# Feed-forward portions and the output projection inside the attention, issued as four products of 32 array columns each

## The chip, the cores and the metric

The kernel runs on one NeuronCore of one Trainium2 chip. The metric is the time of one execution on the device in microseconds. Three runs of the kernel before took 2801.73, 2804.95 and 2811.61 us, a median of 2804.95 us.

## The reference, cut to what matters

x has the shape (4, 2048, 256), float32: four batches of 2048 tokens.

```
xn  = layernorm(x)
x1  = layernorm(xh  + mha(xh,  wq1, wk1, wv1, wo1))      # xh: the first 128 features of xn
x2  = layernorm(xsh + mha(xsh, wq2, wk2, wv2, wo2))      # xsh: the same of holt(xn), a smoothing over the tokens
y   = concat(x1, x2)
out = x + layernorm(y + relu(y @ w_ff1.T + b_ff1) @ w_ff2.T + b_ff2) + relu(xn @ W1 + b1) @ W2 + b2

mha: 8 heads of 16 features; softmax(q k^T / 4) v over all 2048 tokens, the heads side by side, then @ wo.T + bo
```

Each batch has so two attentions of 8 heads, a small network on y (256 to 1024 to 256), and a second, independent one on xn (W1, W2). The change concerns the products of that second network and those with wo.

## The kernel before, in words

**Stages.** For each of the four batches there is a prologue (transposes, projections to q, k and v, the smoothing), the attention of both branches, and the network on y (`nets`). Every engine has its own program, and semaphores tie them together. The middle batches are one loop (`Fori`).

**The attention.** A batch is cut into 16 units (2 branches x 2 groups of 4 heads x 4 chunks of 512 query tokens), and a unit into 16 steps over the key tiles of 128 tokens (kt). In `attention` of `tensor_program` TensorE issues, in this order, for each step kt:

- the scores of step kt + 1 (L1160): 4 products, each with 50 array rows and 128 columns, two of them side by side in the upper and the lower half of the array rows;
- in half of the steps one portion of the second network: in the even units `second_hidden` (L1031), 6 products that make 128 of the 1024 hidden features for 256 tokens; in the odd units `second_out_part` (L1045), 6 products of the second matrix. Each product has all 128 array rows and columns, 256 streamed columns and float16 operands (a value is split into a high and a low part, so three pairs of parts times two halves of the contraction or two hidden blocks);
- in step 8 of each unit but the first, `out_projection` (L1016) of the unit before: 4 products of 128 x 128 on 128 streamed columns in float32, each of which is two instructions in the trace;
- the values of step kt (L1184): for each of the 4 heads one product of 128 array rows and 17 columns (16 features and a column of ones for the sum) on 512 streamed columns, in float32, again two instructions each. Head j writes to the PSUM partitions from 32 j on, so the four lie side by side in the array columns.

The steps with a portion are `NET_KTS` = 0, 2, 4, 6, 10, 12, 14 and 15 (in unit 0 of a batch `FIRST_NET_KTS`), and the projection is in `PROJECTION_KT` = 8. So steps 14, 15 and the next unit's 0 have portions without a step between them.

**What couples the engines.** ScalarE makes one exponential of 128 x 1024 for each half of a step's scores (L584), two per step. The scores cycle through three PSUM slots and the exponentials through four SBUF buffers. The scores of half n wait for the exponential n - 3, and the values of step kt for both exponentials of that step. VectorE takes the portion's result out of the bank `side` (`hidden_half`, L719 to L723; `second_tile`, L731), reads the values of a finished unit (`evict`, L676) before the first values of the next unit may overwrite them, normalises them, and adds the projection to the residual (L713). In its program the work on the last portion of an even unit stands ahead of `evict`.

**Weights.** Each product has a weight load of its own, a separate instruction (PEld in the profile). A matmul's left operand is what is loaded, its right operand what is streamed.

Of the kernel before, what the change touches and what calls it, by code (L numbers as in the profile page):

```python
# [6 lines left out]
B, S, D = 4, 2048, 256  # L7
# [5 lines left out]
P = 128  # L13
# [6 lines left out]
ROW = P // GH  # L20
HB = FF // P
# [150 lines left out]
def build(nc, x, packed, w_ff, w_ffn, out):  # L172
# [8 lines left out]
    with ctx:  # L181
        def sb(name, shape, dt=f32):
            return ctx.enter_context(nc.sbuf_tensor(name, shape, dt))
# [12 lines left out]
        def c(name):  # L196
            return con[:, COLS[name][0]:COLS[name][1]]
# [5 lines left out]
        wo = c("wo").rearrange("p (a g n) -> p a g n", a=2, g=GROUPS)  # L203
# [42 lines left out]
        def fast_programs():  # L246
# [10 lines left out]
            att = sb("att", [P, 2, CHUNK])  # L257
# [42 lines left out]
            o_bank, side = slot[3][:, 0:CHUNK], slot[3][:, CHUNK:]  # L300
# [700 lines left out]

            def tensor_program(pe):

                def out_projection(b, n):
                    a, g, c_ = UNIT_LIST[n]
                    u, i = UNITS2 * b + n, (n + 1) // 2

                    pe.wait_ge(att_ready, u + 1)
                    if n == UNITS2 - 1:
                        pe.wait_ge(net2_read, HT * HALVES * (b + 1))  # L1010
                    elif n % 2:
                        pe.wait_ge(hid2_read, HB * (HALVES * b + i) + 4)
                    else:
                        pe.wait_ge(net2_read, HT * (HALVES * b + i) + 1)
                    for t in range(CT):
                        mm = pe.matmul(side[:, t * P:(t + 1) * P], att[:, n % 2, t * P:(t + 1) * P], wo[:, a, g, :], start=True, stop=True)  # L1016
                    mm.then_inc(out_made, 1)

                def second_hidden(b, i, k):
                    h = HALVES * b + i  # L1020
                    if k == 4 and i > 0:
                        pe.wait_ge(out_read, UNITS2 * b + 2 * i)
                    elif k > 0:
                        pe.wait_ge(hid2_read, HB * h + k)
                    elif i > 0:
                        pe.wait_ge(net2_read, HT * h)
                    bank = side[:, (k % 2) * HALF_TOK:(k % 2 + 1) * HALF_TOK]
                    tok = slice(HALF_TOK * i, HALF_TOK * (i + 1))
                    for n, (w, src) in enumerate(((w1_hi, xt_hi), (w1_hi, xt_lo), (w1_lo, xt_hi))):
                        for f in range(2):  # L1030
                            mm = pe.matmul(bank, w[:, f, k * P:(k + 1) * P], src[:, f, tok], start=(n + f == 0), stop=(n == 2 and f == 1))  # L1031
                    mm.then_inc(hid2_made, 1)

                def second_out_part(b, i, k):
                    h = HALVES * b + i
                    t, first = k // 4, 2 * (k % 4)
                    if k == 0:
                        pe.wait_ge(hid2_read, HB * (h + 1))
                    if k == 4:
                        pe.wait_ge(out_read, UNITS2 * b + 2 * i + 1)  # L1040
                    for m in (first, first + 1):
                        if t == 0:
                            pe.wait_ge(hid2_ready, HB * h + m + 1)
                        for n, (src, w) in enumerate(((hid_hi, w2_hi), (hid_hi, w2_lo), (hid_lo, w2_hi))):
                            mm = pe.matmul(side[:, t * D:(t + 1) * D], src[:, m, t * P:(t + 1) * P], w[:, m, :],  # L1045
                                           start=(m == 0 and n == 0), stop=(m == HB - 1 and n == 2))
                    if first == HB - 2:
                        mm.then_inc(net2_made, 1)

                def prologue(b, before=None):  # L1050
# [20 lines left out]
                    for j in range(4):  # L1071
                        if j == 3 and before is not None:
                            out_projection(before, UNITS2 - 1)

                            pe.wait_ge(out_read, UNITS2 * b)
                        transpose8(j, lambda t: xn[:, 8 * (j % 2) + t, (j // 2) * DH:(j // 2 + 1) * DH])
# [72 lines left out]
                def attention(b):  # L1149
# [15 lines left out]
                    for unit, (a, g, c_) in enumerate(UNIT_LIST):  # L1165
                        u = UNITS2 * b + unit
                        net_kts = FIRST_NET_KTS if unit == 0 else NET_KTS
                        for kt in range(TILES):

                            if kt + 1 < TILES:  # L1170
                                scores(unit, kt + 1)
                            elif unit + 1 < UNITS2:
                                scores(unit + 1, 0)
                            if kt in net_kts:
                                (second_out_part if unit % 2 else second_hidden)(b, unit // 2, net_kts.index(kt))
                            if kt == PROJECTION_KT and unit > 0:
                                out_projection(b, unit - 1)
                            if kt == 0:

                                pe.wait_ge(o_read, u + 1)  # L1180
                            pe.wait_ge(exp_done, STEPS * u + 2 * kt + 2 + 3)
                            for j in range(GH):
                                n = 2 * kt + j // 2
                                mm = pe.matmul(o_bank[ROW * j:ROW * j + DK + 1, :], v_sb[:, a, kt, GH * g + j, :],  # L1184
                                               p_sb[:, n % 4, (j % 2) * CHUNK:(j % 2 + 1) * CHUNK],
                                               start=(kt == 0), stop=(kt == TILES - 1), skip_group_check=True)
                            mm.then_inc(pv_done, 1)
# [62 lines left out]
                def last(b):  # L1250
                    attention(b)
                    out_projection(b, UNITS2 - 1)

                    pe.wait_ge(out_read, UNITS2 * (b + 1))
                    nets(b)
# [919 lines left out]
```

## Time and profile before

| | |
|---|---|
| median of three runs | 2804.95 us |
| the profiled execution | 2801.63 us, its span 2800.0 us |
| attention of the first batch | 120 to 636 us of the span |
| TensorE, products | busy 2600.6 us, 93% |
| ScalarE | busy 2206.4 us, 79% |
| VectorE | busy 1546.7 us, 55% |
| GpSimd | busy 427.1 us, 15% |
| mean granted clock of TensorE | 0.976 |

Times are microseconds unless marked ns. PE is TensorE's products and PEld its weight loads, DVE is VectorE, ACT ScalarE, POOL GpSimd. L1184 is line 1184 of the kernel. "128*17 128x512 f32" in a row of PE means 128 array rows and 17 columns loaded, 512 columns streamed. The durations of single products overlap each other, since they are pipelined; the distance between two starts is the better measure of what one costs, and the prediction uses it.

### The profile page before, as it was taken

What the parts mean: (1) busy time and instruction counts of PE and PEld (TensorE: products, weight loads), DVE (VectorE), ACT (ScalarE), POOL (GpSimd) and SP (SyncE); (2) the same over time, 40 slices, a digit from 0 to 9 for tenths busy, and PEclk for the clock granted to TensorE, in tenths of its full rate; (3) what the DMA queues carried; (4) which work ended last, traced back from release to release, by engine and by line L of the source; (5) the groups of instructions that cost most, each with busy time, mean ns of one, the idle gap of its engine ahead of it and who ended that gap; (6) DMA issues with size and microseconds to landing.
All of it is one profiled execution on the core that took longest, in us unless ns stands there. A gap on an engine that the chain in (4) does not pass through costs nothing.

```text
span 2800.0 us, 53558 instructions
## 1 busy us (share of the span) xinstructions
PE 2600.6 (93%) x19305; PEld 959.3 (34%) x19305; DVE 1546.7 (55%) x3226; ACT 2206.4 (79%) x2409; POOL 427.1 (15%) x404
## 2 busy tenths in 40 slices
PE   2899999998889999999898999999988999999985
PEld 1322222224532222223463222222355222222253
DVE  7554555554764454555375455555558444554566
ACT  1489999993469999998347999999555999999932
POOL 3501000002520100000351010000054010000142
PEclk9999999999999999999899999999999999999998
DMA  3511010002220101000412011000031010100001
GB/s 137 101 39 32 9 32 9 9 5 81 55 77 9 32 9 32 14 8 5 116 31 62 9 32 28 20 9 5 20 101 46 24 32 9 32 9 9 5 27 39
DMA packets 50528, 95.00 MB, mean 34 GB/s; under 512 B 8768, under 2 KB 33344, under 8 KB 49872
## 3 DMA queue, kind: packets, MB, share of 16 engines
q1 hardware_dynamic: 39504, 65.70, 7.3%
q0 software_dynamic: 10752, 25.71, 5.7%
q8 instruction: 167, 2.74, 0.4%
q14 instruction: 105, 0.86, 0.1%
HBM read 57.23 MB, written 34.08 MB: 33 GB/s over the span
## 4 chain that ended last, share of the span: by engine, by line
PE 79%; DVE 7%; POOL 5%; issue 4%; ACT 2%; DMA 1%; DVEq 0%; POOLq 0%; ACTq 0%; SPq 0%
PE slot L1184 35%; PE slot L1160 19%; PE slot L1031 7%; PE slot L1045 6%; POOL p_sb L490 3%; PE slot L1224 3%; PE slot L1016 2%; PE slot L1085 2%; ACT p_sb L584 2%; PE slot L1115 1%; PE slot L1214 1%; POOL k_st L446 1%; POOL q_st L446 1%; DVE stats L652 1%; PE slot L1113 1%
## 5 line engine op out<-in xcount | busy, mean ns | idle before, releaser
L584 ACT ACTIVATE p_sb<-slot 128x1024 f32<-128x1024 f32 x2048 | 1938.2, 1030 | 160.8 <-PE slot L1160 150.0
L1184 PE MATMUL slot<-p_sb,v_sb 128*17 128x512 f32 x8192 | 1082.0, 600 | 12.6 <-ACT p_sb L584 10.7
L1160 PE MATMUL slot<-q_st,k_st 50*128 50x512 f16 x4096 | 625.2, 384 | 19.7 <-issue 10.7
L1160 PEld LDWEIGHTS slot<-q_st,k_st 50*128 50x128 f16 x4096 | 133.8, 94 | 894.7 <-ACT p_sb L584 598.9
L719 DVE TENSOR_SCALAR hid_one<-slot,b_grown 128x256 f32<-128x256 f32 x256 | 123.9, 484 | 297.5 <-PE slot L1031 294.0
L731 DVE SCALAR_TENSOR_TENSOR second<-slot,second 128x256 f32<-128x256 f32 x64 | 27.2, 425 | 401.3 <-PE slot L1045 401.3
L1184 PEld LDWEIGHTS slot<-p_sb,v_sb 128*17 128x17 f32 x8192 | 136.1, 95 | 323.8 <-ACT p_sb L584 196.2
L446 POOL DMA_DIRECT2D k_st<-part_dram x96 | 48.0, 507 | 1188.9 <-PE slot L1184 958.6
L685 DVE RECIPROCAL rden<-den 128x256 f32<-128x256 f32 x128 | 224.4, 1753 | 7.5
L1031 PE MATMUL slot<-xt_parts,w_parts 128*128 128x256 f16 x1536 | 213.0, 275 | 4.5 <-DVE hid_one L719 4.5
L1045 PE MATMUL slot<-w_parts,hid_parts 128*128 128x256 f16 x1536 | 212.1, 274 | 0.0
L1214 PE MATMUL slot<-area,wf_parts 128*128 128x512 f16 x768 | 181.0, 399 | 28.4 <-DVE area L746 22.8
L481 POOL TENSOR_TENSOR resid<-resid,con 128x1024 f32<-128x1024 f32 x16 | 37.7, 2355 | 980.4 <-DVEq L741 980.4
L1224 PE MATMUL slot<-wf_parts,p_sb 128*128 128x256 f16 x1536 | 175.9, 273 | 8.5 <-POOL p_sb L490 8.5
L1031 PEld LDWEIGHTS slot<-xt_parts,w_parts 128*128 128x128 f16 x1536 | 129.6, 98 | 119.1 <-issue 101.6
L1045 PEld LDWEIGHTS slot<-w_parts,hid_parts 128*128 128x128 f16 x1536 | 129.2, 97 | 114.9 <-issue 103.1
L490 POOL TENSOR_TENSOR p_sb<-area,p_sb 128x512 f16<-128x512 f32 x128 | 147.8, 1156 | 118.0 <-ACT p_sb L601 109.9
L1224 PEld LDWEIGHTS slot<-wf_parts,p_sb 128*128 128x128 f16 x1536 | 148.8, 98 | 34.7 <-POOL p_sb L490 13.8
L600 ACT ACTIVATE area<-slot,bf_grown 128x512 f32<-128x512 f32 x128 | 87.9, 687 | 86.5 <-PE slot L1214 69.1
L713 DVE TENSOR_TENSOR resid<-slot,resid 128x512 f32<-128x512 f32 x64 | 44.3, 691 | 188.4 <-PE slot L1016 188.4
L1214 PEld LDWEIGHTS slot<-area,wf_parts 128*128 128x128 f16 x768 | 76.7, 102 | 128.3 <-issue 36.0
L588 ACT ACTIVATE area<-slot 128x1024 f16<-128x1024 f32 x16 | 16.4, 1023 | 128.1 <-PE slot L1199 114.4
(112 smaller groups left out, 2020.3 us busy)
## 6 DMA issues: line engine op xcount, KB each, us to landing
part_dram<-p_sb SPq DMA_DIRECT2D x16, 1024.0 KB, 4.0
k_st<-part_dram POOLq DMA_DIRECT2D x96, 128.0 KB, 5.8
q_st<-part_dram POOLq DMA_DIRECT2D x96, 128.0 KB, 8.1
xn<-x SPq DMA_DIRECT2D x16, 512.0 KB, 6.5
second<-x SPq DMA_DIRECT2D x32, 256.0 KB, 3.5
ffn_dram<-second SPq DMA_DIRECT2D x32, 256.0 KB, 2.0
area<-ffn_dram SPq DMA_DIRECT2D x16, 512.0 KB, 4.9
out<-area SPq DMA_DIRECT2D x16, 512.0 KB, 3.3
```

The lines of the kernel that those rows point to most:

```text
L446: pool.dma_start(stack[at:at + DK, pairs, :], src).then_inc(stack_in[g], 16)
L490: pool.tensor_tensor(h_lo[:, m, :], h_one[:, m % 2, :], h_hi[:, m, :], ALU.subtract).then_inc(hid_ready, 1)
L584: act.activation(p_sb[:, n % 4, :], slot[n % 3][:, :], ACT.Exp, scale=0.25 / GROW ** 2).then_inc(exp_done, 1)
L600: act.activation(h_one[:, m % 2, :], bank, ACT.Relu, bias=bf_grown[:, m:m + 1])
L685: step(dve.reciprocal(rden[:, cols], den[:, cols]))
L719: dve.tensor_scalar(hid_one[:, :], bank, b1_grown[:, k:k + 1], 0.0, ALU.add, ALU.max).then_inc(hid2_read, 1)
L1031: mm = pe.matmul(bank, w[:, f, k * P:(k + 1) * P], src[:, f, tok], start=(n + f == 0), stop=(n == 2 and f == 1))
L1045: mm = pe.matmul(side[:, t * D:(t + 1) * D], src[:, m, t * P:(t + 1) * P], w[:, m, :], start=(m == 0 and n == 0), stop=(m == HB - 1 and n ...
L1160: mm = pe.matmul(slot[at % 3][:, k * CHUNK:(k + 1) * CHUNK], k_st[rows_, pair, kt * P:(kt + 1) * P], q_st[rows_, pair, c_ * CHUNK:(c_ + 1) ...
L1184: mm = pe.matmul(o_bank[ROW * j:ROW * j + DK + 1, :], v_sb[:, a, kt, GH * g + j, :], p_sb[:, n % 4, (j % 2) * CHUNK:(j % 2 + 1) * CHUNK], ...
L1214: mm = pe.matmul(slot[m // 2 % 2][:, (m % 2) * CHUNK:(m % 2 + 1) * CHUNK], w[:, k, m * P:(m + 1) * P], src[:, k * CHUNK:(k + 1) * CHUNK], ...
L1224: mm = pe.matmul(bank[:, t * D:(t + 1) * D], src[:, m, t * P:(t + 1) * P], w[:, m, :], start=(m == 0 and r == 0), stop=(m == HB - 1 and r ...
```

## The change

Inside `tensor_program` a helper `narrow` takes the place of `pe.matmul` in `out_projection`, `second_hidden` and `second_out_part`. It issues one product as four, the r-th with the left operand's columns 32 r to 32 r + 31, and writes to the output's partitions 32 r to 32 r + 31. The streamed operand, the start and stop flags and the arithmetic are the same; so a portion is 24 products and weight loads in place of 6, and a projection 32 in place of 8 in the trace's count. No wait, buffer or order is touched. The scores and the values stay as they are, and so do the prologue and `nets`.

```diff
--- before.py
+++ after.py
@@ -1001,6 +1001,13 @@
 
             def tensor_program(pe):
 
+                def narrow(out, lhs, rhs, start, stop):
+
+                    for r in range(P // ROW):
+                        mm = pe.matmul(out[ROW * r:ROW * (r + 1), :], lhs[:, ROW * r:ROW * (r + 1)], rhs, start=start, stop=stop,
+                                       skip_group_check=True)
+                    return mm
+
                 def out_projection(b, n):
                     a, g, c_ = UNIT_LIST[n]
                     u, i = UNITS2 * b + n, (n + 1) // 2
@@ -1013,7 +1020,7 @@
                     else:
                         pe.wait_ge(net2_read, HT * (HALVES * b + i) + 1)
                     for t in range(CT):
-                        mm = pe.matmul(side[:, t * P:(t + 1) * P], att[:, n % 2, t * P:(t + 1) * P], wo[:, a, g, :], start=True, stop=True)
+                        mm = narrow(side[:, t * P:(t + 1) * P], att[:, n % 2, t * P:(t + 1) * P], wo[:, a, g, :], True, True)
                     mm.then_inc(out_made, 1)
 
                 def second_hidden(b, i, k):
@@ -1028,7 +1035,7 @@
                     tok = slice(HALF_TOK * i, HALF_TOK * (i + 1))
                     for n, (w, src) in enumerate(((w1_hi, xt_hi), (w1_hi, xt_lo), (w1_lo, xt_hi))):
                         for f in range(2):
-                            mm = pe.matmul(bank, w[:, f, k * P:(k + 1) * P], src[:, f, tok], start=(n + f == 0), stop=(n == 2 and f == 1))
+                            mm = narrow(bank, w[:, f, k * P:(k + 1) * P], src[:, f, tok], n + f == 0, n == 2 and f == 1)
                     mm.then_inc(hid2_made, 1)
 
                 def second_out_part(b, i, k):
@@ -1042,8 +1049,8 @@
                         if t == 0:
                             pe.wait_ge(hid2_ready, HB * h + m + 1)
                         for n, (src, w) in enumerate(((hid_hi, w2_hi), (hid_hi, w2_lo), (hid_lo, w2_hi))):
-                            mm = pe.matmul(side[:, t * D:(t + 1) * D], src[:, m, t * P:(t + 1) * P], w[:, m, :],
-                                           start=(m == 0 and n == 0), stop=(m == HB - 1 and n == 2))
+                            mm = narrow(side[:, t * D:(t + 1) * D], src[:, m, t * P:(t + 1) * P], w[:, m, :],
+                                        m == 0 and n == 0, m == HB - 1 and n == 2)
                     if first == HB - 2:
                         mm.then_inc(net2_made, 1)
```

## Rows read from the trace of the kernel before

**Rows 1.** The page's busy time: engine, us, share of the span, instructions.

```profile
PE 2600.6 (93%) x19305; PEld 959.3 (34%) x19305; DVE 1546.7 (55%) x3226; ACT 2206.4 (79%) x2409; POOL 427.1 (15%) x404
```

**Rows 2.** The chain of waits that ended last, by engine and line.

```profile
PE 79%; DVE 7%; POOL 5%; issue 4%; ACT 2%; DMA 1%; DVEq 0%; POOLq 0%; ACTq 0%; SPq 0%
PE slot L1184 35%; PE slot L1160 19%; PE slot L1031 7%; PE slot L1045 6%; POOL p_sb L490 3%; PE slot L1224 3%; PE slot L1016 2%; PE slot L1085 2%; ACT p_sb L584 2%; PE slot L1115 1%; PE slot L1214 1%; POOL k_st L446 1%; POOL q_st L446 1%; DVE stats L652 1%; PE slot L1113 1%
```

**Rows 3.** Windows, two units: window length, busy of PE, PEld, DVE, ACT, POOL; clock.

```profile
354.34:417.70 63.36, 63.10 (x498) 18.60 (x496) 33.74 (x77) 60.57 (x64) 6.98 (x14) 1.00 0.22 35
```

**Rows 4.** Timeline of PE, steps with and without a portion (start, us, line).

```profile
402.40 0.61 PE L1160 MATMUL slot<-q_st,k_st 50*128 50x512 f16 x4
402.94 0.83 PE L1031 MATMUL slot<-xt_parts,w_parts 128*128 128x256 f16 x6
403.70 1.05 PE L1184 MATMUL slot<-p_sb,v_sb 128*17 128x512 f32 x8
404.69 0.61 PE L1160 MATMUL slot<-q_st,k_st 50*128 50x512 f16 x4
405.22 1.05 PE L1184 MATMUL slot<-p_sb,v_sb 128*17 128x512 f32 x8
406.20 0.60 PE L1160 MATMUL slot<-q_st,k_st 50*128 50x512 f16 x4
...
409.02 0.63 PE L1184 MATMUL slot<-p_sb,v_sb 128*17 128x512 f32 x4
```

**Rows 5.** Timeline of PE: the projection and the values behind it.

```profile
430.65 1.16 PE L1016 MATMUL slot<-con,att 128*128 128x128 f32 x8
431.74 1.05 PE L1184 MATMUL slot<-p_sb,v_sb 128*17 128x512 f32 x8
```

**Rows 6.** Timeline of PE in the network on y, then in the smoothing.

```profile
744.64 1.04 PE L1199 MATMUL slot<-con,resid 128*128 128x128 f32 x8
745.51 2.78 PE L1224 MATMUL slot<-wf_parts,p_sb 128*128 128x256 f16 x24
...
658.32 1.03 PE L1111 MATMUL slot<-xn,con 128*2 128x128 f32 x8
659.29 1.12 PE L1113 MATMUL slot<-con,state 2*128 2x512 f32 x2
```

**Rows 7.** Timeline of PE, two narrow windows: the values' two rounds.

```profile
403.70 0.62 PE L1184 MATMUL slot<-p_sb,v_sb 128*17 128x512 f32 x4
404.14 0.61 PE L1184 MATMUL slot<-p_sb,v_sb 128*17 128x512 f32 x4
```

**Rows 8.** Products and weight loads by line (busy us, mean ns of one).

```profile
L1184 PE MATMUL slot<-p_sb,v_sb 128*17 128x512 f32 x8192 | 1082.0, 600 | 12.6 <-ACT p_sb L584 10.7 <-DVE o_sb L676 0.9
L1031 PEld LDWEIGHTS slot<-xt_parts,w_parts 128*128 128x128 f16 x1536 | 129.6, 98 | 119.1 <-issue 101.6 <-DVE hid_one L719 5.5
L1111 PEld LDWEIGHTS slot<-xn,con 128*2 128x2 f32 x96 | 7.2, 84 | 4.4 <-issue 2.7
```

**Rows 9.** Timeline of PE: the densest run of products.

```profile
88.39 1.06 PE L1140 MATMUL slot<-k_diag,p_sb 128*128 128x128 f16 x16
```

**Rows 10.** Timeline of ACT in the steps of rows 4.

```profile
405.19 1.94 ACT L584 ACTIVATE p_sb<-slot 128x1024 f32<-128x1024 f32 x2
407.02 1.95 ACT L584 ACTIVATE p_sb<-slot 128x1024 f32<-128x1024 f32 x2
```

**Rows 11.** Timeline where an even unit ends and an odd one begins.

```profile
412.83 0.83 PE L1031 MATMUL slot<-xt_parts,w_parts 128*128 128x256 f16 x6
413.59 1.05 PE L1184 MATMUL slot<-p_sb,v_sb 128*17 128x512 f32 x8
413.70 0.48 DVE L719 TENSOR_SCALAR hid_one<-slot,b_grown 128x256 f32<-128x256 f32 x1 [1.01 <-PE slot L1031]
415.34 0.73 DVE L676 STREAM_SHUFFLE o_sb<-slot 128x512 f32<-128x512 f32 x1
416.20 1.05 PE L1184 MATMUL slot<-p_sb,v_sb 128*17 128x512 f32 x8 [0.26 <-ACT p_sb L584]
```

## Prediction

> **What bounds the kernel now.** I read the page's busy time first. TensorE is busy 93% of the span and ScalarE 79% [rows 1]; that is near for both, so the averages don't decide. The chain of waits does: 79% of it is TensorE's own, with the values (L1184) and the scores (L1160) at 35% and 19%, and the three lines of the change (L1031, L1045, L1016) at 7%, 6% and 3%; ScalarE's exponentials are only 2% [rows 2]. Then one even and one odd unit in the windows: of 63.36 us TensorE is busy 63.10 and ScalarE 60.57 [rows 3]. In the attention TensorE sets the pace, with ScalarE 3 us behind in 63. The attention is 32 such pairs of units, 32 x 63.36 = 2028 of the 2800 us.
>
> The timeline shows what a step is made of. A step with a portion: scores from 402.40, portion from 402.94, values from 403.70, next scores from 404.69; so 0.54 + 0.76 + 0.99 = 2.29 us. A step without one: 404.69, 405.22, 406.20, so 1.51 us [rows 4]. The two together take 3.80. The projection's step has a piece of 1.09 us instead of 0.76 [rows 5]. Added up, a unit is 16 x 1.52 + 8 x 0.76 + 1.09 = 31.5 us, against 63.36 / 2 = 31.7 measured [rows 3]: nearly everything is TensorE's work laid end to end.
>
> **What a change of the array's arrangement costs.** Work of one arrangement follows without a gap: eight transposes of 128 x 128 start at 744.64 and the next line's products at 745.51, which is 0.109 us for each of the eight [rows 6]. Eight products with 2 columns (L1111), followed by products with 2 array rows (L1113), take 659.29 - 658.32 = 0.97 us; eight at 0.109 are 0.87, and 0.10 us is left [rows 6]. The portion shows the same: 0.76 us is six at 0.11 and a rest of 0.10 [rows 4]. The projection's eight at 0.109 are 0.87 and the rest 0.22 [rows 5]. I read the 0.10 us as the price of each change of arrangement. A step with a portion now pays it three times (scores, portion, values). If the portion stands in the arrangement of the values, it pays twice.
>
> **The change part by part.**
>
> *Removed:* one change of arrangement behind each portion and each projection.
>
> *Added:* 18 products with their loads to each portion, 24 to each projection. The sum needs the time of four narrow products side by side. The values are such a case: their first four start at 403.70 and the second four at 404.14 [rows 7], and the four together span 0.62 us where one lasts 0.60 [rows 7, 8]; so all four run at once and start within some 0.02 us. A round takes 0.44 us for 512 float32 columns, four times the 0.11 of a wide product with a quarter of its columns [rows 5 to 7]: no loss from being four. The low end of a round in the portion is so 0.11 us, that of a wide product. For the high end I let each of the four pay the fixed part of a product on its own: 256 columns at 2.4 GHz, the upper level, are 0.107 us of the 0.11, so four times 0.003 makes 0.12. I take the middle, 0.115. The portion becomes 6 x 0.115 = 0.69 us (saves 0.07), the projection 8 x 0.115 = 0.92 us (saves 0.17). Both ends again: 0.66 to 0.72 and 0.88 to 0.96.
>
> Nothing before the change shows three or more narrow products in a row on each quarter of the array with four quarters in use. The nearest rows bound it above: the densest run of products is 16 in 1.06 us, at most 0.066 each with the last one's tail [rows 9]. If each narrow product needed a slot of about 0.056 us of TensorE's own (1.06 less a tail of about 0.2, over 15), a portion would take 24 x 0.056 = 1.34 us. From below, products of full width say 0.65. I take the row that is nearest in kind, the values.
>
> *Gross sum:* a pair of units has 16 portions and 2 projections, 16 x 0.07 + 2 x 0.17 = 1.46 us.
>
> *What is late next, the exponentials.* In a step without a portion the values start as soon as the second exponential is there: scores start at 404.69, ScalarE at 405.19, its fourth exponential from there ends at 407.02 + 1.95 = 408.97, and the values start at 409.02 [rows 4, 10]. That is 4.33 us. TensorE's own way from 404.69 to 409.02 is 0.53 + 0.98 + 0.54 + 0.76 + 0.98 + 0.53 = 4.32 us. The two ways end together, so a shorter portion meets a wait. From these values to the scores that start ScalarE again is TensorE's work alone, 3.26 us less the saving s. Two pairs of steps take then 4.33 + 3.26 - s = 7.59 - s, one pair 3.80 - s/2: half of the saving is lost. A pair of units has 12 such pairs of steps (1-2, 3-4, 5-6, 9-10, 11-12, 13-14 in each unit), which loses 12 x 0.035 = 0.42 us. Steps 15 and 0, which have portions next to each other, and step 8 are TensorE's alone. ScalarE's throughput doesn't bind: four exponentials start 0.91 apart (407.02 less 405.19, halved) [rows 10], 3.66 us per pair of steps against 3.77.
>
> *What is late next, VectorE.* At the end of an even unit VectorE takes the last portion at 413.70, then reads the unit's values from 415.34 for 0.73 us, and the next values start at 416.20 although the portion before them, 0.54 + 0.76 us behind 414.57, was done at 415.87 [rows 4, 11]. This chain starts at the last portion's results, which come no earlier, so the savings of the portions in steps 15 and 0 are lost there: 2 x 0.07 = 0.14 us. At the end of an odd unit no portion's result stands before the reading.
>
> *Net:* 1.46 - 0.42 - 0.14 = 0.90 us per pair of units, 32 x 0.90 = 29 us. The prologue and the network on y have no edit. The profiled execution took 2801.6 us and would take 2773; the median is 3.3 us above it, so I forecast 2776. With the low ends (0.66 and 0.88) it is 16 x 0.10 + 2 x 0.21 - 12 x 0.05 - 0.20 = 1.22, 39 us, 2766; with the high ends (0.72 and 0.96) 0.64 + 0.26 - 0.24 - 0.08 = 0.58, 19 us, 2786. The forecast's own range is 2760 to 2792.
>
> **The rivals.**
>
> *Each narrow product needs its own slot* (the slower side). With 0.056 us a product a portion takes 1.34 us (+0.58) and a projection 32 x 0.056 = 1.79 us (+0.70): 16 x 0.58 + 2 x 0.70 = 10.7 us per pair, all on TensorE's path, +342 us, about 3147. It decides from 0.76 / 24 = 0.032 us a product on. For it: no run of products denser than 0.056 is in the trace. Against: the four values start within 0.02 us [rows 7, 8], though these may have been waiting in a queue. A step with a portion would hold 36 products in 2.2 us, where 18 stand now.
>
> *The weight loads come out of hiding.* A wide load lasts 98 ns beside a product of 110 [rows 4, 8]. If a quarter's next load can't run beside its product, a round is 0.11 + 0.098 = 0.21 us, a portion 1.25 (+0.49), a projection 1.66 (+0.57): 9.0 us per pair, +288 us, 3093. Against: products of 2 columns, which change their weights each time, keep 0.109 us with loads of 84 ns [rows 6, 8]; they use one quarter only. The Trainium skill speaks for this rival: "TensorE: Matmul & The Clock Gate", "The mechanism", says that a weight load overlaps products in flight only where the row group differs, which four column products don't; and "TensorEngine Tiling (Array Packing)", "Restrictions", that column tiling switches the fast weight load off. By that rule a portion would be the 1.25 us of this rival; the rows with 2 columns disagree with its strict form, and none here shows it for 32 columns and four quarters.
>
> *The change doesn't do what it says.* The values load 17 columns, the portion 32; if these aren't one arrangement, the 0.10 us stays: a portion 0.79 (+0.03), a projection 1.02 (-0.07), so 0.48 - 0.14 = +0.34 us per pair, +11 us, 2816.
>
> *A round takes 0.125 us or more.* A portion is then 0.75, and what is left is the projections': within 0.3% of 2805.
>
> *The exponentials take all of it.* If in the 12 pairs of steps nothing comes through and the boundary loses as above, 2 x 0.07 + 2 x 0.17 = 0.48 us per pair are left, 15 us, 2790.
>
> **How the numbers follow.** About 0.3% (8 us) is what can be told from no change. Forecast 0.59; all but 15 us eaten by the exponentials 0.08; rounds of 0.125 us 0.08; arrangement not shared 0.06; own slot 0.11; loads exposed 0.08. Faster is 0.59 + 0.08 = 0.67, the same 0.08, slower 0.25. The two large rivals hold 0.19 and are left out of the range; it reaches from 2752, for rounds at the low end with less lost to the waits, to 2820, which takes in the unshared arrangement.
>
> **What would show it.** In the profile after, a portion's 24 products should take 0.69 us from its first start to that of the values, with the values behind it without the 0.10 us; the projection 0.92. TensorE should wait for ScalarE in about every second step without a portion, for some 0.07 us, and a pair of units should take about 62.5 us. Portions above 0.76 us make the forecast wrong, and so would a pair of units that stays at 63.4 with portions of 0.69.

## The result and the profile after

The changed kernel takes 2761.0 us in the median (four runs, 2756.3 to 2761.5), the kernel before 2804.2 in the same comparison: a ratio of 0.984, with a 95% interval of 0.982 to 0.986. It is 43 us faster, where 29 were forecast. The profiled execution took 2760.5 us.

The page's busy time after answers to [rows 1]; the chain by line to [rows 2]. L1007 is the line of the helper `narrow`, which now holds portions and projections; L1167 are the scores and L1191 the values.

```profile
PE 2554.9 (93%) x30057; PEld 1013.5 (37%) x30057; DVE 1543.7 (56%) x3226; ACT 2185.3 (79%) x2409; POOL 428.9 (16%) x404
...
PE 77%; DVE 10%; POOL 6%; issue 4%; ACT 2%; DMA 1%; DVEq 0%; POOLq 0%; ACTq 0%; SPq 0%
```

There are 10752 more products (18 in each of 512 portions, 24 in each of 64 projections), and TensorE is busy 46 us less. VectorE's share of the chain went from 7% to 10%. Most of that is the boundary below: in this kernel the chain runs through VectorE there for 2.0 us per pair of units, 2.3% of the span over 32 pairs; before, it ran through an exponential.

Two units in the windows (length, busy time of PE, PEld, DVE, ACT, POOL) and a stretch of PE's timeline with a portion, a step without one, and a projection, against [rows 3 to 5]:

```profile
350.21:412.23 62.02, 61.38 (x834) 20.08 (x832) 33.73 (x77) 59.88 (x64) 7.01 (x14) 1.00 0.22 36
```

```profile
351.22 0.60 PE L1167 MATMUL slot<-q_st,k_st 50*128 50x512 f16 x4
351.76 0.84 PE L1007 MATMUL slot<-w_parts,hid_parts 128*32 128x256 f16 x24
352.42 1.03 PE L1191 MATMUL slot<-p_sb,v_sb 128*17 128x512 f32 x8
353.39 0.61 PE L1167 MATMUL slot<-q_st,k_st 50*128 50x512 f16 x4
354.04 1.05 PE L1191 MATMUL slot<-p_sb,v_sb 128*17 128x512 f32 x8
355.02 0.61 PE L1167 MATMUL slot<-q_st,k_st 50*128 50x512 f16 x4
...
363.05 1.08 PE L1007 MATMUL slot<-con,att 128*32 128x128 f32 x32
363.94 1.04 PE L1191 MATMUL slot<-p_sb,v_sb 128*17 128x512 f32 x8
```

The portion's 24 products take 0.66 us from their start to that of the values (0.76 before), six rounds at 0.11 with nothing behind them. The values after a portion take 0.97 us instead of 0.99. So portion and values save together 0.11 to 0.12 us (0.759 to 0.665 us and 0.985 to 0.965 us in the medians of a batch). The projection takes 0.89 instead of 1.09. The step without a portion is longer than before: the values start 0.65 us after the scores (354.04 less 353.39) where it was 0.53 [rows 4]. It happens in six of the fourteen steps of a pair of units that have neither a portion nor a projection.

A pair of units takes 62.02 us where it took 63.36 [rows 3], 1.34 us less. This holds for the first three batches, whose attention stands in the loop. The last batch, which is written out behind the loop, gained more: its pairs went from 63.20 us (2254.09 to 2317.29) to 61.40. The step without a portion shows why; its values start 0.57 us behind the scores there, not 0.65:

```profile
2224.28 0.74 DVE L676 STREAM_SHUFFLE o_sb<-slot 128x512 f32<-128x512 f32 x1
...
2285.68 0.74 DVE L676 STREAM_SHUFFLE o_sb<-slot 128x512 f32<-128x512 f32 x1
...
2352.54 0.61 PE L1167 MATMUL slot<-q_st,k_st 50*128 50x512 f16 x4
2353.11 1.05 PE L1191 MATMUL slot<-p_sb,v_sb 128*17 128x512 f32 x8
```

From the first scores to the last values the four attentions take 507.4, 499.6, 499.7 and 492.5 us, where they took 516.7, 509.8, 509.7 and 506.9: 44 us less in all. The rest of this execution is 3 us longer than in the profiled execution before, at a mean granted clock of 0.971 against 0.976. So the whole is not 32 x 1.34 us, though that is 43 too. The loop's batches gave 29.5 us where 24 x 1.34 would be 32, since the first unit of an attention gained next to nothing, and the last one gave 14.4 where 8 x 1.34 would be 11. That the simple product meets the measured 43 is partly luck.

The end of an even unit, against [rows 11], all engines:

```profile
408.00 1.03 PE L1191 MATMUL slot<-p_sb,v_sb 128*17 128x512 f32 x8
408.23 0.48 DVE L719 TENSOR_SCALAR hid_one<-slot,b_grown 128x256 f32<-128x256 f32 x1 [0.90 <-PE slot L1007]
...
409.50 0.84 PE L1007 MATMUL slot<-w_parts,hid_parts 128*32 128x256 f16 x24
409.85 0.01 DVE L676 LOAD_MASK_SELECT o_sb<-slot  x1 [0.35 <-DVE hid_parts L723]
409.87 0.74 DVE L676 STREAM_SHUFFLE o_sb<-slot 128x512 f32<-128x512 f32 x1
410.74 1.05 PE L1191 MATMUL slot<-p_sb,v_sb 128*17 128x512 f32 x8 [0.40 <-DVE o_sb L676]
```

From values to values there are 2.74 us here; it was 2.61 (416.20 less 413.59, [rows 11]). TensorE's own work in such a step is 2.17 now and was 2.28, so the wait for VectorE grew from 0.33 to 0.57 us. (In the last batch it grew from 0.17 to 0.41.) The row before names an exponential as the releaser, [0.26 <-ACT p_sb L584]; the run that moves the reading in the kernel before, below, shows that it was the reading.

### The profile page after: what moved, and what is told of

Its sections match the earlier page's. It is cut to its first block, busy times and chain, and to the rows that moved or that the text cites. A ratio compares the mean times of both kernels' runs of the same rounds, so it can differ in the third digit from the quotient of the medians.

```text
span 2759.0 us, 75062 instructions
## 1 busy us (share of the span) xinstructions
PE 2554.9 (93%) x30057; PEld 1013.5 (37%) x30057; DVE 1543.7 (56%) x3226; ACT 2185.3 (79%) x2409; POOL 428.9 (16%) x404
## 3 DMA queue, kind: packets, MB, share of 16 engines
q0 software_dynamic: 10752, 25.71, 5.7%
## 4 chain that ended last, share of the span: by engine, by line
PE 77%; DVE 10%; POOL 6%; issue 4%; ACT 2%; DMA 1%; DVEq 0%; POOLq 0%; ACTq 0%; SPq 0%
PE slot L1191 33%; PE slot L1167 19%; PE slot L1007 16%; POOL p_sb L490 3%; PE slot L1231 3%; PE slot L1092 2%; PE slot L1122 1%; DVE o_sb L676 1%; DVE rs L642 1%; ACT p_sb L584 1%; DVE hid_parts L721 1%; POOL k_st L446 1%; POOL q_st L446 1%; DVE stats L652 1%; DVE hid_one L719 1%
## 5 line engine op out<-in xcount | busy, mean ns | idle before, releaser
L584 ACT ACTIVATE p_sb<-slot 128x1024 f32<-128x1024 f32 x2048 | 1916.6, 1029 | 138.6 <-PE slot L1167 135.9
L1191 PE MATMUL slot<-p_sb,v_sb 128*17 128x512 f32 x8192 | 1073.2, 598 | 22.3 <-DVE o_sb L676 11.5
L1167 PE MATMUL slot<-q_st,k_st 50*128 50x512 f16 x4096 | 624.6, 384 | 19.1 <-issue 10.9
L1167 PEld LDWEIGHTS slot<-q_st,k_st 50*128 50x128 f16 x4096 | 127.2, 94 | 894.9 <-ACT p_sb L584 721.9
L1191 PEld LDWEIGHTS slot<-p_sb,v_sb 128*17 128x17 f32 x8192 | 180.3, 97 | 240.8 <-ACT p_sb L584 214.9
L1007 PE MATMUL slot<-xt_parts,w_parts 128*32 128x256 f16 x6144 | 215.6, 275 | 5.8 <-DVE hid_one L719 5.8
L1007 PE MATMUL slot<-w_parts,hid_parts 128*32 128x256 f16 x6144 | 214.7, 274 | 0.0
L1007 PEld LDWEIGHTS slot<-xt_parts,w_parts 128*32 128x32 f16 x6144 | 141.2, 96 | 112.6 <-issue 103.7
L1007 PEld LDWEIGHTS slot<-w_parts,hid_parts 128*32 128x32 f16 x6144 | 141.2, 96 | 106.8 <-issue 104.8
L588 ACT ACTIVATE area<-slot 128x1024 f16<-128x1024 f32 x16 | 16.4, 1024 | 128.8 <-PE slot L1206 108.7
```

Of the source, the lines that this page charges most:

```text
L584: act.activation(p_sb[:, n % 4, :], slot[n % 3][:, :], ACT.Exp, scale=0.25 / GROW ** 2).then_inc(exp_done, 1)
L1007: mm = pe.matmul(out[ROW * r:ROW * (r + 1), :], lhs[:, ROW * r:ROW * (r + 1)], rhs, start=start, stop=stop, skip_group_check=True)
L1167: mm = pe.matmul(slot[at % 3][:, k * CHUNK:(k + 1) * CHUNK], k_st[rows_, pair, kt * P:(kt + 1) * P], q_st[rows_, pair, c_ * CHUNK:(c_ + 1) ...
```

## The experiments

Four questions were open: whether it is the arrangement that pays, what each part is worth, where the rest of TensorE's saving went, and how near a limit of products or instructions is. The theory (A in the expectations) is that the array needs 0.10 us to change its arrangement, that four narrow products run at once at 0.11 us a round, and that portions in the values' arrangement save one change each.

**The portions alone, and the projection alone.**

```diff
-                        mm = narrow(side[:, t * P:(t + 1) * P], att[:, n % 2, t * P:(t + 1) * P], wo[:, a, g, :], True, True)
+                        mm = pe.matmul(side[:, t * P:(t + 1) * P], att[:, n % 2, t * P:(t + 1) * P], wo[:, a, g, :], start=True, stop=True)
```

> The changed kernel with the projection (out_projection) wide again, the portions narrow. Theory A: what is saved is the 0.10 us that the array takes to change its arrangement between a portion and the values behind it, four narrow products run at once at 0.11 us a round. Then portion and values stay at 1.63 us together (1.74 before), and the projection goes back from 1.87 with its values to 2.07. Of the 1.34 us saved per pair of units 2 x 0.20 = 0.40 go, 0.94 x 32 = 30 us faster than before, about 2774. Rival B, a narrow product is faster wherever it stands: the same here, so this run only sizes the parts. Rival C, the projection made the difference: within 5 us of before.

Measured: 2771.6 us against 2806.5 of before, ratio 0.988 (0.986 to 0.990), 35 us faster. A pair of units takes 62.44 us in its trace, 0.92 less than before; one pair in the first batch took 63.16:

```profile
286.21 0.73 DVE L676 STREAM_SHUFFLE o_sb<-slot 128x512 f32<-128x512 f32 x1
348.64 0.73 DVE L676 STREAM_SHUFFLE o_sb<-slot 128x512 f32<-128x512 f32 x1
411.81 0.74 DVE L676 STREAM_SHUFFLE o_sb<-slot 128x512 f32<-128x512 f32 x1
```

The other way round, with `pe.matmul` in the two portions and `narrow` in the projection:

> The changed kernel with the portions wide again, the projection narrow. Theory A: 2 x 0.20 us per pair of units, nothing of it lost since step 8 waits for nothing but TensorE, 32 x 0.40 = 13 us faster than before, about 2791; with the run of the portions alone the two parts add up to the 43 us of the change. If the waits for the exponentials make them overlap, the two add up to more than 43.

Measured: 2792.3 us, ratio 0.995 (0.993 to 0.996), 14 us faster; a pair takes 62.95, 0.41 less:

```profile
286.50 0.73 DVE L676 STREAM_SHUFFLE o_sb<-slot 128x512 f32<-128x512 f32 x1
349.44 0.73 DVE L676 STREAM_SHUFFLE o_sb<-slot 128x512 f32<-128x512 f32 x1
```

The two parts, 0.92 and 0.41, add up to the 1.34 of the change. Rival C falls. The times themselves, 35 and 14, add up to 49 where the change gave 43; their intervals (28 to 38, and 10 to 20) take in both. The traces decide: the four attentions are 31.3 and 11.2 us shorter, 42.5 together, against the change's 43.9. So the two savings don't overlap.

**Two products of 64 columns.** This separates the arrangement from narrowness.

```diff
-                    for r in range(P // ROW):
-                        mm = pe.matmul(out[ROW * r:ROW * (r + 1), :], lhs[:, ROW * r:ROW * (r + 1)], rhs, start=start, stop=stop,
+                    for r in range(P // HALF):
+                        mm = pe.matmul(out[HALF * r:HALF * (r + 1), :], lhs[:, HALF * r:HALF * (r + 1)], rhs, start=start, stop=stop,
```

> The changed kernel with each product as two of 64 array columns in place of four of 32. Theory A (arrangement): 64 columns are neither the scores' nor the values' arrangement, so the 0.10 us behind each portion stays, a portion takes 0.76 us as before and the time is that of before, 2804 within 6 us. Rival B (a narrower product, or its shorter weight load, is faster in itself): about half of the gain comes, 2783, or all of it, 2761.

Measured: 2803.5 us against 2806.5, ratio 0.999 (0.998 to 1.000); a pair of units takes 63.46, 0.10 more than before. In PE's timeline the portion of twelve products takes 0.78 us, and the scores after the values start 0.98 us later:

```profile
402.89 0.60 PE L1167 MATMUL slot<-q_st,k_st 50*128 50x512 f16 x4
403.42 0.85 PE L1007 MATMUL slot<-xt_parts,w_parts 128*64 128x256 f16 x12
404.20 1.05 PE L1191 MATMUL slot<-p_sb,v_sb 128*17 128x512 f32 x8
405.18 0.60 PE L1167 MATMUL slot<-q_st,k_st 50*128 50x512 f16 x4
```

For the portions halving the width gives nothing; it gives only where the width puts the products into the neighbours' arrangement. Rival B is out for them. The 64 columns are in this an arrangement of their own. The projection did gain a little: 1.02 us in this trace, between the 1.09 of the wide and the 0.90 of the narrow one. No run tells what that 0.06 is.

**Narrow products with wide neighbours.** The control from the other side: the second product of `nets`.

```diff
-                                    mm = pe.matmul(bank[:, t * D:(t + 1) * D], src[:, m, t * P:(t + 1) * P], w[:, m, :],
-                                                   start=(m == 0 and r == 0), stop=(m == HB - 1 and r == 2))
+                                    mm = narrow(bank[:, t * D:(t + 1) * D], src[:, m, t * P:(t + 1) * P], w[:, m, :],
+                                                m == 0 and r == 0, m == HB - 1 and r == 2)
```

> The changed kernel with the second product of the network on y (nets, L1231) narrow as well: 1536 products become 6144, their neighbours stay wide. Theory A (only a shared arrangement pays): the rounds stay at 0.11 us, and each group of narrow products now pays 0.10 us for the arrangement at its start and its end, twice more where the transposes of the next chunk stand in between; some 60 changes in all, at most 6 us: 2761 to 2768. Rival (a narrow product is faster in itself by a tenth): 1536 x 0.01 = 15 us less, 2746. Rival (a stream of narrow products longer than a portion's 24 runs into a limit of its own): rounds above 0.115 us show in the trace, and the time is above 2770.

Measured: 2760.1 us, ratio to before 0.984 (0.982 to 0.986), the same as the changed kernel's and just under the 2761 to 2768 that I expected. Its timeline, and the same place in the changed kernel behind it:

```profile
731.14 5.75 PE L1007 MATMUL slot<-wf_parts,p_sb 128*32 128x256 f16 x204 [0.19 <-POOL p_sb L490]
736.83 1.09 PE L1206 MATMUL slot<-con,resid 128*128 128x128 f32 x8
737.85 2.81 PE L1007 MATMUL slot<-wf_parts,p_sb 128*32 128x256 f16 x96
```

```profile
728.72 5.74 PE L1231 MATMUL slot<-wf_parts,p_sb 128*128 128x256 f16 x51 [0.32 <-POOL p_sb L490]
734.30 1.04 PE L1206 MATMUL slot<-con,resid 128*128 128x128 f32 x8
735.17 2.78 PE L1231 MATMUL slot<-wf_parts,p_sb 128*128 128x256 f16 x24
```

204 narrow products take 5.69 us to the next line, 51 wide ones 5.58: the same 0.109 a round and 0.11 us for the change behind it. The eight wide transposes, between narrow neighbours, take 1.02 us instead of 0.87. So the price of an arrangement appears where there was none. A stream of 200 narrow products loses no pace. The time doesn't tell these changes from nothing: some 60 of them are 6 us at most, and the kernel's own executions lie 5 us apart.

**Where the rest of the saving went: the exponentials.** In both kernels every exponential was cut to 512 of its 1024 columns; the others are left out, so what these two compute is wrong and only their times count.

```diff
-                        act.activation(p_sb[:, n % 4, :], slot[n % 3][:, :], ACT.Exp, scale=0.25 / GROW ** 2).then_inc(exp_done, 1)
+                        act.activation(p_sb[:, n % 4, 0:CHUNK], slot[n % 3][:, 0:CHUNK], ACT.Exp, scale=0.25 / GROW ** 2).then_inc(exp_done, 1)
```

> The changed kernel with exponentials of 512 of their 1024 columns; the other half of each is left out, so ScalarE's part of a step falls from 1.83 to about 1.0 us. Theory A: of what the change saves on TensorE's pieces (16 x 0.11 + 2 x 0.20 = 2.16 us per pair of units) 0.66 is lost in six steps without a portion, whose values wait 0.11 us for their exponentials, and the rest at VectorE's reading of a finished even unit. With short exponentials the 0.66 comes back: a pair of units takes 61.3 to 61.4 us (62.02 in the changed kernel). Rival: these waits are something else, and the pair stays at 62.0.

> The kernel before with exponentials of 512 of their 1024 columns, the other half left out. Theory A: before the change TensorE waits for no exponential, so a pair of units stays at 63.2 to 63.4 us, and between this and the changed kernel with the same cut the change is worth 1.9 to 2.0 us per pair in place of 1.34. Rival (ScalarE bounds part of the kernel before too): clearly below 63.2.

Measured by the distance of two readings of even units (L676) in each trace. The changed kernel with short exponentials:

```profile
344.38 0.73 DVE L676 STREAM_SHUFFLE o_sb<-slot 128x512 f32<-128x512 f32 x1
...
405.72 0.74 DVE L676 STREAM_SHUFFLE o_sb<-slot 128x512 f32<-128x512 f32 x1
```

The kernel before with short exponentials:

```profile
351.38 0.74 DVE L676 STREAM_SHUFFLE o_sb<-slot 128x512 f32<-128x512 f32 x1
...
414.74 0.74 DVE L676 STREAM_SHUFFLE o_sb<-slot 128x512 f32<-128x512 f32 x1
```

61.34 and 63.36 us. Before the change ScalarE cost next to nothing: with its work halved, the pair stayed at 63.36. (Two pairs in seven had been 63.49; here none is.) After the change its waits cost 62.02 - 61.34 = 0.68 us per pair in the three batches of the loop and 0.20 in the last, 24 x 0.68 + 8 x 0.20 = 18 us in all. Without these waits the change would have been worth 2.02 us per pair. (Single runs: 2735.6 and 2800.1 us.)

**Where the rest went: VectorE's order.** The reading of an even unit's values is put ahead of the cast and the subtraction of the last hidden block. `hidden_parts` holds these two; nothing is left out.

```diff
+                    if k < HB - 1:
+                        hidden_parts(b, i, k)
+
+                def hidden_parts(b, i, k):
+                    n = HB * (HALVES * b + i) + k
                     dve.wait_ge(hid2_read, n + 1)
...
                         if n > 0:
                             evict(b, n - 1)
+                        if n % 2:
+                            hidden_parts(b, i, HB - 1)
```

> The changed kernel with VectorE's reading of a finished even unit (evict) moved ahead of the cast and the subtraction of the last hidden block; the work is the same. Theory A: at the end of every even unit TensorE now waits 0.40 us for that reading, whose start stands 1.64 us behind the last portion's results; with 0.75 us of other VectorE work out of the way it starts at the end of the values and its result is there as TensorE arrives. The wait goes, up to 0.40 us per pair of units, 32 x 0.40 = 13 us, less what the exponentials take back (they start 0.82 us late there): 5 to 13 us faster than the changed kernel, 2748 to 2756. Rival: the wait is really for the exponentials, and the time stays at 2761.

Measured: 2744.8 us against 2806.5, ratio 0.978 (0.976 to 0.980), and 16 us less than the changed kernel's 2761.0, more than the 5 to 13 that I expected. (The two medians come from different comparisons; within the traces the four attentions are 17 us shorter.) A pair takes 61.44 us in the loop, one pair in each of its batches 61.78, and 60.96 in the last batch. The boundary in its timeline (L1198 the values, L1174 the scores, L1014 the portion):

```profile
404.47 1.03 PE L1198 MATMUL slot<-p_sb,v_sb 128*17 128x512 f32 x8
404.69 0.48 DVE L719 TENSOR_SCALAR hid_one<-slot,b_grown 128x256 f32<-128x256 f32 x1 [0.89 <-PE slot L1014]
405.43 0.61 PE L1174 MATMUL slot<-q_st,k_st 50*128 50x512 f16 x4
405.72 0.74 DVE L676 STREAM_SHUFFLE o_sb<-slot 128x512 f32<-128x512 f32 x1
405.97 0.84 PE L1014 MATMUL slot<-w_parts,hid_parts 128*32 128x256 f16 x24
406.63 1.03 PE L1198 MATMUL slot<-p_sb,v_sb 128*17 128x512 f32 x8
```

Values to values are 2.16 us, TensorE's own work; 2.74 - 2.16 = 0.58 is the whole gain of a pair of 61.44. I had priced the wait at the 0.40 us that the trace gives as idle time of PE. The idle time counts from the end of the portion's record, 0.84 us behind its start, but the next line can start 0.665 us behind it; so the idle time that the row shows is too small by some 0.17 us, and the distance of the starts is the measure.

The same move on the kernel before:

> The kernel before with VectorE's reading of a finished even unit ahead of the last hidden block's cast and subtraction, the products wide. Theory A: the wait for that reading at the end of an even unit was 0.33 us before the change (2.61 us from values to values where TensorE's work is 2.28) and 0.57 after it, so moving the reading gives 0.33 x 32 = 10 us here, about 2794, against the 16 to 18 us that it gave on the changed kernel: the change had turned 0.24 us per pair of units of its saving into this wait. Rival (the move gains by other means, the same in both): 16 to 18 us here too, 2788.

Measured: 2794.1 us against 2805.3, ratio 0.996 (0.995 to 0.997), 11 us faster; most pairs take 63.02, 0.34 less. The wait at the boundary is gone, 2.29 us from values to values:

```profile
412.94 1.05 PE L1191 MATMUL slot<-p_sb,v_sb 128*17 128x512 f32 x8
...
415.23 1.05 PE L1191 MATMUL slot<-p_sb,v_sb 128*17 128x512 f32 x8
```

The wait was so worth 0.34 before the change and 0.58 after: 0.24 us per pair, 8 us in all, of what TensorE saved ended in this wait.

**Is a round spent on its four products?** `for r in range(P // ROW)` became `for r in range(1)`: three quarters of every portion and projection are left out, so the result is wrong. The one run took 2756.5 us.

> The changed kernel with only the first of the four narrow products each time; the other three quarters of each portion and projection are left out. Theory A (the four run at once): a portion still takes 0.66 us from its first product to the values, within 0.02, and a pair of units 62.0. Rival (part of a round is spent on issuing four): a portion is shorter, down to 0.64.

A portion of six products that are alone in their quarter takes 0.66 us (406.02 to 406.68), and a pair 61.86:

```profile
406.02 0.72 PE L1007 MATMUL slot<-xt_parts,w_parts 128*32 128x256 f16 x5
406.47 0.62 PE L1191 MATMUL slot<-p_sb,v_sb 128*17 128x512 f32 x3
406.57 0.27 PE L1007 MATMUL slot<-xt_parts,w_parts 128*32 128x256 f16 x1
406.68 1.02 PE L1191 MATMUL slot<-p_sb,v_sb 128*17 128x512 f32 x5
```

Three products of the values start at 406.47, in quarters that the portion left free, before the portion's last one at 406.57. So quarters of one arrangement run independently of each other, and the three others cost next to nothing: the pair is 0.16 us shorter without them (I expected no difference), some 0.01 us a portion.

**How dense can they be?** Each hidden portion as 48 products on 128 streamed columns, the result the same.

```diff
+                    for q in range(2):
+                        half = slice(q * P, (q + 1) * P)
...
+                                mm = narrow(bank[:, half], w[:, f, k * P:(k + 1) * P], src[:, f, tok][:, half], n + f == 0, n == 2 and f == 1)
```

> The changed kernel with the 24 products of each hidden portion (even units) split into 48 that stream 128 columns in place of 256; the same result. It asks how densely narrow products can follow. Theory A without a floor: 12 rounds of 0.056 us, a hidden portion stays near 0.67. Rival (own slot for each product): a floor of more than 0.014 us a product shows; at 0.025 us a hidden portion takes 48 x 0.025 = 1.2 us, and the time rises by about 128 x 2 x 0.54 = 130 us at most; at 0.056 it takes 2.7 us.

PE's timeline has both things that came out of it: a portion at full pace, and one that broke off.

```profile
406.32 0.85 PE L1007 MATMUL slot<-xt_parts,w_parts 128*32 128x128 f16 x48
407.00 1.03 PE L1193 MATMUL slot<-p_sb,v_sb 128*17 128x512 f32 x8
```

```profile
393.46 0.80 PE L1007 MATMUL slot<-xt_parts,w_parts 128*32 128x128 f16 x43
...
397.89 0.40 PE L1007 MATMUL slot<-xt_parts,w_parts 128*32 128x128 f16 x5 [3.64 <-issue]
...
398.00 1.99 PE L1193 MATMUL slot<-p_sb,v_sb 128*17 128x512 f32 x8
```

At full pace 48 products with their loads take 0.68 us, 0.014 us each; no floor for a single product showed. But the kernel took 2793.7 us (one run), 33 more than the changed one. A pair of units without a stop takes 62.10, so the longer portions explain 32 x 0.08 = 3 us. The rest stands in the loop's three batches, and most of it in seven stops in the middle of a group, with no release by any engine: 20.6 us as the trace counts them, five of 3.4 to 4.4 us between two starts and two of 1.5 and 0.8. Behind a stop the values can run at half pace (1.99 us for 1.05). That is the clock: TensorE's granted clock fell to 0.50, the lower level of 1.2 GHz, around the end of four of the five long stops and stayed there for 3.4 to 6.8 us. The stop at 394 us and what follows it, in the windows (the same columns as [rows 3]; the last three are the granted clock, the DMA engines' busy share and GB/s):

```profile
394.00:397.90 3.90, 0.26 (x21) 0.09 (x10) 0.00 (x0) 1.69 (x2) 0.00 (x0) 0.93 0.51 68
397.90:400.00 2.10, 2.10 (x15) 0.41 (x17) 1.20 (x3) 0.00 (x0) 0.00 (x0) 0.50 0.00 0
```

What stopped TensorE is argued, not shown: I take it for the supply of instructions. The packets of queue q8, which the page calls "instruction", rose from 167 before to 251 with the change and 299 here; the stops fall between two instructions of one straight run; and each of the seven ended 1.2 to 1.7 us after a packet of q8 had landed. Six of them fell while GpSimd's transfers of the next k and q (queue q0) kept the DMA engines busy, as the 0.51 above shows, and the last batch has such transfers and no stop. No run separates the density of instructions from these transfers.

## Why the prediction was right

**The price of an arrangement, 0.10 us, and that a shared one saves it:** right, and shown from both sides: by the 64 columns, which gain nothing, and by the narrow products in `nets`, which lose 0.11 and 0.15 us at their neighbours. Two places go beyond this price. The values behind a narrow portion gain 0.02 us. And for the projection the sum took off the whole rest of 0.22 us, where one change at 0.10 was what it had argued for. That came true, 0.20 per projection, but it was luck, and why a wide float32 projection loses twice what a portion loses stays open.

**The round at 0.115 us:** too high. It is 0.11, my low end: the portion takes 0.66 and not 0.69, the projection 0.89 and not 0.92. The four fixed parts that I added don't add up; the run with one quarter has the same 0.66. With the 0.02 of the values this made the forecast 15 us too cautious: gross 16 x 0.115 + 2 x 0.20 = 2.24 us per pair of units, where I had 1.46. With my low ends the sum was 1.22 net and 2766 us, 5 from the measured time.

**Half of a portion's saving lost to the exponentials in the pairs of steps:** the mechanism was right. The wait stands in about every second step without a portion, 0.11 us long, and 0.68 us per pair of units come back with short exponentials; the rule of s/2 with s = 0.115 says 12 x 0.0575 = 0.69. But I took it to hold in all 32 pairs. It rests on two ways of 4.33 and 4.32 us that end together, read in the first batch. In the last batch ScalarE's way ends sooner: the wait after the change is 0.03 us, and only 0.20 us per pair are lost. So its eight pairs gained 1.8 us each and not 1.34. What makes ScalarE's way shorter outside the loop no run shows.

**The savings of steps 15 and 0 lost to VectorE at the boundary:** right, and for the reason given, that its chain starts at the last portion's results. Measured 0.24 us per pair, 2 x 0.12, where the 0.14 came from s = 0.07. The net is 2.26 - 0.68 - 0.24 = 1.34, where 2.26 is what the pairs differ by with these waits taken off: 63.36 - 0.33 = 63.03 wide, 62.02 - 0.57 - 0.68 = 60.77 narrow. TensorE's pieces, added up from their medians, give the same two numbers, 63.03 and 60.78, so the 2.26 isn't only what the subtraction leaves.

**The rivals:** own slot for each product, weight loads exposed, unshared arrangement and a round of 0.125 us or more are all refuted by the portion's 0.66 us. That the exponentials take all of it is refuted by the 0.92 us per pair that the portions alone gave. The rule of the Trainium skill's "TensorE: Matmul & The Clock Gate", "The mechanism", by which a load overlaps products only in another row group, doesn't hold in its strict form here: loads of 96 ns changed the weights of every quarter each 110 ns, in the run of 48 products each 57, and the rounds kept their pace. That the fast weight load is off in column tiling, as the Trainium skill's "TensorEngine Tiling (Array Packing)", "Restrictions", says, cost nothing that shows: a narrow load lasts 96 ns, a wide one 98 [rows 8]. Whether it is off here no run tells.

## What to carry to other kernels

Where different products alternate on TensorE, count the changes of arrangement (rows x columns of the array that a product takes) from the distance of starts, and see whether a wide product can be written as side by side narrow ones in its neighbour's arrangement; 64 columns between neighbours of 32 are worth nothing. When the pacing engine gets shorter, look at once at the waits that end just as it arrives: here two of them took 0.92 of 2.26 us, and a change in another engine's order, which cost nothing, brought 16 us on top of the change's 43. Read a pair of units in every stage before multiplying: the last batch, outside the loop, behaved otherwise. Four times a portion's instructions were free but for one stop, eight times were not.

## What the runs showed that I had not expected

- Quarters of the array in one arrangement overtake each other: values started in three quarters 0.10 us before the last product of a portion in the fourth.
- The stops of up to 4.4 us when a hidden portion had 96 instructions, and the fall of the granted clock to the lower level behind four of them; the run with the portions alone has a smaller one (0.73 us) in one pair of units, 63.16 us instead of 62.44. The changed kernel has none: its pairs of the first three batches lie between 62.01 and 62.07 us, those of the last at 61.39 to 61.40.
- Float32 products in four quarters (0.109 us a round of 128 columns) cost no more than float16 ones with 256, though a wide float32 projection lost 0.22 us behind its eight rounds and the narrow one 0.02.
